# Graph attention and experts in one kernel: units of 128 places instead of 256, and TensorE's selections in quarters between the scatters

## The reference

```python
x = x + conv2d(bfp_quantize(layernorm_c(x)), bfp_quantize(weight), bias)
t = tokens(x)                                     # [50176, 64]
h = (layernorm(t) @ W_gat).reshape(M, 4, 4)
e = leaky_relu(a_src[src] + a_dst[dst], 0.2)      # for each edge and each node's own loop
alpha = segment_softmax(e, dst)
agg = segment_sum(h[src] * alpha[:, :, None], dst)
scores = layernorm(agg + b_gat).reshape(M, 4, 4).mean(1)
w, chosen = softmax(top_2(scores))
out = sum over 4 experts of gate_e * (gelu(t @ W1[e] + b1[e]) @ W2[e] + b2[e])
result = x + out
```

## Time and profile before

| | us |
|---|---|
| median of 3 runs | 4160.18 (4157.43 to 4185.01) |
| profiled execution, its own time | 4170.91 |
| its span, first to last instruction | 4169.2 |
| busy: PE, DVE, POOL | 2785.7, 2803.7, 2784.5 |
| busy: ACT | 1968.9 |
| granted TensorE clock, mean | 0.794 |

### The profile page before, as it was taken

How to read it: one execution, slowest core, us unless ns; L and a number is a source line. 1 busy time by engine, 2 the same in 40 slices (tenths; PEclk the granted TensorE clock), 3 DMA queues, 4 the chain that set the end, 5 groups by cost and what they waited for, 6 DMA issues and landing times.

```text
span 4169.2 us, 59836 instructions
## 1 busy us (share of the span) xinstructions
PE 2785.7 (67%) x19158; PEld 2168.6 (52%) x19194; DVE 2803.7 (67%) x4674; ACT 1968.9 (47%) x3257; POOL 2784.5 (67%) x2785
## 2 busy tenths in 40 slices
PE   5488433368885288777777677777677676677685
PEld 1255322245653276555556565556556565555563
DVE  8877999988885367555665656565666565565664
ACT  0011000001110478666766677666667676666773
POOL 3000388878875777777777777777777777777771
PEclk8799655568886579788888888888878888788887
DMA  1133211169998922222222222222222222222293
GB/s 54 31 93 94 64 45 45 45 70 122 120 116 116 115 46 57 51 51 51 56 51 46 52 54 56 51 51 51 49 43 55 51 56 51 51 51 46 51 46 26
DMA packets 383251, 253.27 MB, mean 61 GB/s; under 512 B 302146, under 2 KB 337538, under 8 KB 382596
## 3 DMA queue, kind: packets, MB, share of 16 engines
q1 hardware_dynamic: 295284, 220.70, 25.4%
q0 software_dynamic: 87552, 29.20, 9.7%
q10 hardware_dynamic: 144, 0.00, 0.0%
HBM read 179.40 MB, written 70.24 MB: 60 GB/s over the span
## 4 chain that ended last, share of the span: by engine, by line
POOL 49%; issue 16%; DVE 1%; PE 1%; DMA 1%; ACT 0%; DVEq 0%; SPq 0%; ACTq 0%; POOLq 0%
POOL gath L1228 49%; DMA gath<-tab_d,src_no 0%; DMA blk_row<-blk_d 0%; PE A L1400 0%; PE C L1377 0%; PE A L1408 0%; PE A L1390 0%; ACT nodes L1292 0%; PE C L1360 0%; DVE A L1623 0%; DVE nodes L1624 0%; DVE spread L1538 0%; DVE spread L1456 0%; DVE spread L1459 0%; DVE acc L1551 0%
## 5 line engine op out<-in xcount | busy, mean ns | idle before, releaser
L1228 POOL DMA_INDIRECT gath<-tab_d,src_no x2116 | 2003.1, 947 | 644.7 <-issue 644.7
L1377 PE MATMUL C<-spread,lo_hot 128*128 128x160 f32 x4360 | 850.6, 361 | 589.0 <-DVEq L1553 377.2
L1377 PEld LDWEIGHTS C<-spread,lo_hot 128*128 128x128 f32 x4360 | 779.2, 236 | 720.6 <-DVEq L1553 488.0
L493 POOL DMA_INDIRECT edge_d<-run_slots,slots x544 | 674.2, 1239 | 602.3 <-ACT run_slots L692 439.2
L1258 ACT ACTIVATE lo_gap<-lane,lo_less 128x128 bf16<-128x128 f32 x2192 | 667.5, 388 | 4.4
L1551 DVE TENSOR_TENSOR acc<-acc,C 128x160 f32 x1090 | 349.7, 321 | 378.8 <-PE C L1377 162.1
L1360 PEld LDWEIGHTS C<-damp,lo_hot_t 128*128 128x128 f32 x4384 | 534.4, 198 | 114.0 <-issue 114.0
L1360 PE MATMUL C<-damp,lo_hot_t 128*128 x4384 | 544.4, 280 | 53.8 <-ACT lo_hot_t L1249 36.8
L605 PE MATMUL C<-wide_rec,hot_lo 128*128 128x136 f16 x2048 | 271.9, 305 | 300.3 <-DVE wide_rec L893 300.3
L605 PEld LDWEIGHTS C<-wide_rec,hot_lo 128*128 128x128 f16 x2048 | 242.2, 123 | 352.9 <-DVE wide_rec L893 294.3
L1538 DVE TENSOR_TENSOR spread<-hi_hot,C 128x2560 f32<-128x2560 f32 x137 | 386.4, 2821 | 4.7
(11 more groups left out here) (284 smaller groups left out, 3435.8 us busy)
## 6 DMA issues: line engine op xcount, KB each, us to landing
lo_rows<-lo_d SPq DMA_DIRECT2D x137, 512.0 KB
gath<-tab_d,src_no POOLq DMA_INDIRECT x2116
pixels<-in_x SPq DMA_DIRECT2D x32, 392.0 KB, 6.4
src<-in_x SPq DMA_DIRECT2D x32, 392.0 KB, 9.3
nodes<-t_d SPq DMA_DIRECT2D x98, 128.0 KB, 2.8
nodes<-x_d SPq DMA_DIRECT2D x98, 128.0 KB, 2.9
out<-nodes SPq DMA_DIRECT2D x784, 16.0 KB
edge_d<-run_slots,slots POOLq DMA_INDIRECT x544
```

The lines of the kernel that those rows point to most:

```text
L493: pool.indirect_dma_start(edge_d, bass.IndirectOffsetOnAxis(ap=slots[:, k, c:c + 1], axis=0), run_slots[:, k, c * RUN:(c + 1) * RUN, :].re ...
L1228: pool.indirect_dma_start(gath[:, g % BUFS, j, :], None, node_d if g < BUFS else tab_d, bass.IndirectOffsetOnAxis(ap=src_no[:, t:t + 1], a ...
L1377: mm = pe.matmul(C[:, bank, at:at + HI * VALS], lo_hot[:, g % UNROLL, u * U + j, :], spread[:, u * U + j].rearrange("p h v -> p (h v)"), s ...
```

## The change

A unit becomes one tile of 128 places (`U = 1`), a group 16 units, still 16 tiles, in eight pairs of two tiles. `MAX_UNITS` is 2132 then, `NG` 134, and the tiles are 2132 instead of 2180. Each tile's sums go through their own addition on VectorE. The register loads of block numbers double. The selection is cut in quarters (`QUARTERS`); TensorE's order in a group becomes: scatters of pairs 0 and 1, `up`, scatter of pair 2, a quarter, scatter 3, a quarter, scatter 4, a quarter, scatter 5, a quarter, scatters 6 and 7, `down`, `up`, `down`. The raw list has runs in 32 rows instead of 64 and is loaded four times (`PARTS_U = 4`); it is longer than `lo_hot`, so it lies over `lo_hot` and `hi_hot` together (`hots`). To make room the temporaries of `choose` move into the memory of `na`, and `row_i` into that of `acc`.

```diff
-U = 2
-UNIT_RUN_BITS = 6
+U = 1
+UNIT_RUN_BITS = 5
-UG = 8
+UG = 16
...
-                n = PLACES * RUN * FIELDS // 8
-                for k in range(8):
+                n = PLACES * RUN * FIELDS // 16
+                for k in range(16):
...
-                pool.wait_ge(s["pads_written"], 8 * 16)
+                pool.wait_ge(s["pads_written"], 16 * 16)
...
-            lo_hot = tb("lo_hot", [P, UNROLL, G, P])
-            hi_hot = tb("hi_hot", [P, UNROLL, G, HI])
+            hots = tb("hots", [P, UNROLL * G * (P + HI)])
...
-            mine_2 = tb("mine", [P, 2 * HI, FEAT])
-            square_2 = tb("square", [P, 2 * HI, FEAT])
-            half_2 = tb("half_sum", [P, 2 * HI, FEAT // 2])
+            na_row = na[:].rearrange("p q f -> p (q f)")
+            mine_2, square_2 = (na_row[:, k * 2 * HI * FEAT:(k + 1) * 2 * HI * FEAT].rearrange("p (q f) -> p q f", f=FEAT) for k in range(2))
...
+                QUARTERS = 4
+
+                def pick_dst(g, part):
+
+                    first, n = part * UG // QUARTERS, UG // QUARTERS
+                    qs = unit_blocks(pe, g, first, n)
+                    if part == 0:
                         pe.wait_ge(s["lo_hot_t_ready"], g + 1)
                         if g:
                             pe.wait_ge(s["picked_read"], g)
-                    for t in range(half * G // 2, (half + 1) * G // 2):
+                    for t in range(first * U, (first + n) * U):
...
-                    mm.then_inc(s["picked_ready"], 1)
+                    if part % 2:
+                        mm.then_inc(s["picked_ready"], 1)
...
-                    scatter(g, range(0, PAIRS // 2))
+                    scatter(g, range(0, 2))
                     for step in due[0:1]:
                         up(*step)
-                    scatter(g, range(PAIRS // 2, PAIRS))
-                    if g + 2 < NG:
-                        pick_dst(g + 2, 0)
+                    for w in range(2, PAIRS):
+                        scatter(g, range(w, w + 1))
+                        if g + 2 < NG and w < 2 + QUARTERS:
+                            pick_dst(g + 2, w - 2)
                     for step in due[0:1]:
                         down(*step)
                     for step in due[1:2]:
                         up(*step)
-                    if g + 2 < NG:
-                        pick_dst(g + 2, 1)
                     for step in due[1:2]:
                         down(*step)
```

More of the change, by code:

```diff
@@ L1064, in build @@
             amax_d = tb("amax_d", [HEADS, HEADS])
-            lo_hot = tb("lo_hot", [P, UNROLL, G, P])
-            hi_hot = tb("hi_hot", [P, UNROLL, G, HI])
+            hots = tb("hots", [P, UNROLL * G * (P + HI)])
+            lo_hot = hots[:, 0:UNROLL * G * P].rearrange("p (k t l) -> p k t l", k=UNROLL, t=G)
+            hi_hot = hots[:, UNROLL * G * P:UNROLL * G * (P + HI)].rearrange("p (k t h) -> p k t h", k=UNROLL, t=G)
             lo_rows = tb("lo_rows", [P, LO_BUFS, G * P], BF16)
@@ L1079, in build @@
             gate = tb("gate", [P, 4, HI, EXPERTS])
-            mine_2 = tb("mine", [P, 2 * HI, FEAT])
-            square_2 = tb("square", [P, 2 * HI, FEAT])
-            half_2 = tb("half_sum", [P, 2 * HI, FEAT // 2])
+            na_row = na[:].rearrange("p q f -> p (q f)")
+            mine_2, square_2 = (na_row[:, k * 2 * HI * FEAT:(k + 1) * 2 * HI * FEAT].rearrange("p (q f) -> p q f", f=FEAT) for k in range(2))
+            half_2 = na_row[:, 4 * HI * FEAT:5 * HI * FEAT].rearrange("p (q f) -> p q f", f=FEAT // 2)
+            beats_2 = na_row[:, 5 * HI * FEAT:5 * HI * FEAT + 4 * HI * EXPERTS * EXPERTS].rearrange("p (k q e f) -> p k q e f", k=2, q=2 * HI, e=EXPERTS)
             stat_2 = tb("stat", [P, 2 * HI, EXPERTS])
@@ L1087, in build @@
             root_2 = tb("root", [P, 2 * HI, 2])
-            beats_2 = tb("beats", [P, 2, 2 * HI, EXPERTS, EXPERTS])
             rank_2 = tb("rank", [P, 2 * HI, EXPERTS])
@@ L1136, in steps_due @@
                 return [(j, e) for j in range(NB) for e in range(EXPERTS) if STEP_AT[j * EXPERTS + e] == g]
-            raw = lo_hot[:].rearrange("p b t l -> p (b t l)").bitcast(F16)[:, 0:PLACES * RUN * FIELDS]
-            RAW_WORDS = PLACES * RUN * FIELDS // 2
+            raw = hots[:].bitcast(F16)[:, 0:PLACES * RUN * FIELDS]
             @block.sync
@@ L1350, in _ @@
                 pe.matmul(A[:, 3, 0:HEADS], ones[0:HEADS, :], amax_d[:], start=True, stop=True).then_inc(s["amax_spread"], 1)
-                def pick_dst(g, half):
-                    qs = unit_blocks(pe, g, half * UG // 2, UG // 2)
-                    if half == 0:
+                QUARTERS = 4
[3 more added lines that the diff above has]
+                    if part == 0:
                         pe.wait_ge(s["lo_hot_t_ready"], g + 1)
@@ L1358, in pick_dst @@
                             pe.wait_ge(s["picked_read"], g)
-                    for t in range(half * G // 2, (half + 1) * G // 2):
+                    for t in range(first * U, (first + n) * U):
                         mm = pe.matmul(C[:, 0, t * HI * HEADS:(t + 1) * HI * HEADS], lo_hot_t[:, t, :],
-                                       damp[:, bass.ds(qs[t // U - half * UG // 2], HI), :].rearrange("p h f -> p (h f)"), start=True, stop=True)
-                    mm.then_inc(s["picked_ready"], 1)
+                                       damp[:, bass.ds(qs[t // U - first], HI), :].rearrange("p h f -> p (h f)"), start=True, stop=True)
+                    if part % 2:
+                        mm.then_inc(s["picked_ready"], 1)
                 def scatter(g, pairs):
@@ L1414, in _ @@
                 for g in range(2):
-                    for half in range(2):
-                        pick_dst(g, half)
+                    for part in range(QUARTERS):
+                        pick_dst(g, part)
                 for g in range(NG):
                     due = steps_due(g)
-                    scatter(g, range(0, PAIRS // 2))
+                    scatter(g, range(0, 2))
                     for step in due[0:1]:
                         up(*step)
-                    scatter(g, range(PAIRS // 2, PAIRS))
-                    if g + 2 < NG:
-                        pick_dst(g + 2, 0)
+                    for w in range(2, PAIRS):
+                        scatter(g, range(w, w + 1))
+                        if g + 2 < NG and w < 2 + QUARTERS:
+                            pick_dst(g + 2, w - 2)
                     for step in due[0:1]:
@@ L1446, in _ @@
                 mixed_i = spread[:].rearrange("p t h v -> p (t h v)").bitcast(I32)[:, 0:TILES]
-                row_i = lo_hot[:].rearrange("p b t l -> p (b t l)").bitcast(I32)[:, RAW_WORDS:RAW_WORDS + TILES]
+                row_i = acc[:].rearrange("p q v -> p (q v)").bitcast(I32)[:, 0:TILES]
                 def field(v, dt):
```

## The result

The changed kernel takes 4981.65 us, the median of 4 runs (4974.17 to 5000.78), against 4160.09 (4157.43 to 4185.01): a ratio of 1.197, 95% interval 1.194 to 1.200. The profiled execution took 4981.14, its span is 4979.4. Forecast were 4780 us, 4280 to 5060.

The account below looks back on a forecast made before the run. GpSimd's gathers were taken to set the pace, 20.0 us a group. After the change, 11.85 us plus a 13.1 us stretch make a 24.95 us turn; 133 turns, 3318 us, with start and end give 4792, forecast as 4780 (4280 to 5060).

Parts of the forecast that it names:

- Its signs: Expected in the profile: gathers wait for `rows_used`, additions wait 3 to 8 us a group for scatters, mean clock near 0.65.
- What bounds the kernel: Second half: GpSimd's gathers set the pace, 20.0 us a group; VectorE and TensorE may lose only 3.1 us.
- The turn beside the stretch: Loop from one `spread_out` to the next, without first addition to last one's end: 11.85 us.
- The pauses: TensorE waits twice a group: 2.6 us before the first addition's hand-over, about 3 after `down`; both lower the clock.
- The stretch at either level: First addition to last one's end, per group: 9.4 us at full clock, 10.2 with register loads; 15.2 at low clock.
- the uncovered register loads of a quarter: TensorE loads four block numbers before each selection quarter; some 0.2 us each stays uncovered, raising 9.4 us to 10.2.
- How many stretches at which level: Addition stretches: 26 of 134 groups low at 15.2 us, half falling at 14.1, remaining 30% full at 10.2; mean 13.1.
- one pause after another: TensorE: in 30% of groups one pause follows another and the burst between restores the clock, stretch 10.2 us.
- The start: Ahead of the loop: list loaded four times, 10.6 us, plus copies, 2.63 us; 13 us taken, 3 to 25 open.
- Full clock: Rival, chance 0.28: TensorE keeps full clock in the loop; stretch 10.2, turn 22.05, time 4407 us, 4396 against the median.
- VectorE alone: Rival, chance 0.08: selection quarters hidden, VectorE's additions set the stretch, 8.4 us; turn 20.25, time 4168, no change.
- Gathers still set the pace: Rival, chance 0.06: stretch under 8.1 us, so GpSimd's 48 fewer gathers show; time 4124 us, 1.1% less.

Follow-up runs that it names:

- The order alone: Kernel before, units of 256 kept, with the two selection halves moved behind scatters 2 and 3: 4179.7 us, 1.003.
- the units alone: Changed kernel with units of 128 but TensorE's old order, both selection halves behind the last scatter: 4356.56 us, 1.047.
- the kernel with unread matmuls: Changed kernel plus matmuls nobody reads in both TensorE pauses (10 ahead of scatter 2, 65 behind a `choose`, 12 behind a lone `down`): 4458.13 us, 1.071.
- the units alone with unread matmuls: Units of 128 in TensorE's old order, plus 10 matmuls nobody reads ahead of scatter 2, 65 behind a `choose`: 4344.31 us, 1.045.
- the 12 matmuls behind `down`: Changed kernel plus 12 matmuls nobody reads in the second pause only, behind a lone `down`: 4901.34 us, 1.170.

## Why the prediction was right, and where its size was off

The sign, the mechanism and the range held; 4780 was 4% short, and the result lies nearer to the upper end, 5060, at which every stretch is low. Its signs came: the additions wait 7.2 us a group for scatters (3 to 8 forecast), the waits for gathers are gone, and the mean granted clock is 0.70 (0.65 forecast). By its own steps:

- **What bounds the kernel.** Right: 3.1 us a group of slack and no more. The order alone used 2.3 of it, which cost 0.3%; the units alone used it up.
- **The turn beside the stretch.** Forecast 11.85, measured 11.89 (26.46 less a mean stretch of 14.57). That it is so close is partly luck: the 11.85 carries the wait of 36.82 us for the first one-hots, 0.27 a turn, which in the changed kernel stands inside the first stretch (52.2 us); the rest is 0.3 larger than forecast. Inside it block numbers cost 0.49 more instead of 0.35 (0.80 to 1.29 us), and the gates' wait is 0.67 instead of 0.73 (85.2 us in 127.5 groups).
- **The pauses.** The first was forecast at 2.6 us and is 2.83 in the median. The second, forecast at about 3 in every group, stands in 70 of 132 only, with a median of 2.05 us; in the others the `up` and `down` of a second step fill it.
- **The stretch at either level.** 9.4 forecast at the full clock, 9.48 measured; 15.2 at the low one, 15.2 to 15.4 measured. The 0.2 us for the uncovered register loads of a quarter, which made it 10.2, was wrong: 2.3 us of idle time is left before all selection loads from 1500 to 4850 us, where the earlier trace rows had 57.5. At the full clock too the stretch is the sum without them.
- **How many stretches at which level: the term that was mis-sized.** I let 30% run at the full clock, half lose it about 1 us in (14.1) and 20% be low from the start (15.2). Measured are 18 of 133 under 10 us (14%), 8 of 10 to 14, and 107 of 14 and over, 75 of those of 15 and over. The mean stretch is 14.57, not 13.1: 1.47 of the 1.51 us by which the turn was short, of which 0.28 is the wait in the first stretch; and 133 x 1.51 = 201 us.
- **When the clock fell.** By the granted clock, without the first group: in 57 it was low when scatter 2 began (15.3 us on average); in 57 it fell after that, 0.9 us later on average and 2.2 at most (14.7 us); 18 kept it. In no stretch of 12 us or more did it come back before the end of the last scatter. Of the 83 first pauses of 2.4 to 3.1 us, 21 ended at the low clock, 56 were followed by a fall, and 6 by neither, so the length of a pause alone doesn't tell when the clock falls. Of the 18 that kept it, 12 had a first pause of only 0.9 to 1.7 us, because the scatters in front had run at the low clock themselves, 1.9 to 2.5 us instead of 1.35: for these the forecast of one pause after another was right, but they are a tenth and not 30%. The prediction also took both pauses for the long waits of which the Trainium skill speaks ("TensorE: Matmul & The Clock Gate", section "HAM oscillation — how this bites in real kernels"), so that by the rule alone every stretch would be low. The waits that the section describes are longer than the pauses here, so by it alone these pauses needn't lower the clock; the rows decide, and behind 77 of the 83 it was low or fell.
- **The start.** Forecast 13 us, measured 1.1 (first `spread_out` at 1404.6 against 1403.5). The parts were there: the chain's wait for the list and `blk_row` grew from 12.30 to 22.08 us (9.8; 10.6 forecast), and the copies ahead of the first gather from 2.63 to 8.32 (5.7; 2.6 forecast). But the copies had a cover that I missed: VectorE next waits for `nodes`, 18.37 us in the trace of before, 6.10 in this one (the row below), so their price doesn't show. And the wait for the list and `blk_row` began at 1314.6 instead of 1322.1 in this execution; the first `spread_out` lies between 1397 and 1426 in the profiled executions. So 12 us of the forecast are missing, and 4792 + 201 - 12 = 4981. These 12 us and the 0.7 us too much in 10.2 (some 28 us over 30% of the turns) made up for a part of the mis-sized term, by chance.

```profile
1373.51 4.07 DVE L1487 TENSOR_REDUCE amax<-nodes 128x4 f32<-128x1568 f32 x1 [6.10 <-DMA nodes<-node_d]
```

- **Rivals.** *Full clock* was priced at 4396, with 10.2; the kernel with unread matmuls, 4458, is its nearest likeness, with 28 stretches still at 10 us or over, and some 4365 without what the 27 behind the first cost. *VectorE alone* was priced too low: the units alone with unread matmuls have its stretch (8.56 against 8.4) and take 4344 instead of 4168, since their turn over all groups is 12.97 us beside the stretch (21.61 - 8.64), not 11.85. With the old order the wait for the gates doesn't become shorter but longer, 1.44 us (167.8 in 117 groups) instead of the 0.73 that I took: 0.7 of the 1.12. The block numbers are 0.14 more; the other 0.3 I haven't found. *Gathers still set the pace* needed a stretch under 8.1; the shortest was 8.14, and with 13.4 us beside it.

What stays open: what decides whether the clock falls within a pause, behind it or not at all, why the 12 matmuls behind `down` help as much as they do, and whether the part of the turn beside the stretch could be made shorter; no run tried that.

## What to carry to other kernels

Before work is moved into an engine's idle time, ask who waits for what stands behind it in that engine's order: work moved out of a place where nobody waited cost 0.3% while another resource had 3 us of slack, and some 15% more when a second edit had used that slack up, nearly all of it through the clock. Price TensorE's work at the clock that it will have behind the pauses that the change makes, and look in the row behind each pause, not at the mean. Where a shorter stretch doesn't show in the time, look for it in the next wait of the same two engines.

## What the runs showed of the hardware that I had not expected

- A 16-bit to 32-bit copy of 32 partitions x 2144 elements takes 2.08 us, where 64 x 2192 takes 1.31: half the partitions and no more elements in each, 1.6 times as long. The copies from f16 that follow take as long (8.31 for four). Why is open. VectorE in order of time at the start of the loop's phase:

```profile
1337.05 8.32 DVE L1459 CAST spread<-hots 32x2144 int32<-32x2144 uint16 x4
```

- The clock stayed at 0.50 through some 13 us (2614.66 to 2628.2) in which the trace shows no idle time of TensorE, made of pairs of scatter and quarters of selection; here a busy TensorE was no sign of the full clock. And it can fall while TensorE is busy: at 3484 us, 2 us after a pause of 2.83.
- Matmuls that nobody reads cost the kernel before no time that could be measured (1.000), as its slack took them, and gave the changed one 10.5% of its time back, though TensorE did more work.
- Register loads ahead of an instruction of VectorE: 0.50 us for one number, 0.80 for eight, 1.29 for sixteen.
